# Attention output projection: three high/low products in place of one plain float32 product

## The chip, the cores and the metric

The kernel runs on one core of one Trainium2 chip. The metric is the device time of one execution in microseconds. The profiled execution is one execution of the same program, recorded by the hardware profiler; PE is TensorE, PEld its weight loads, DVE VectorE, ACT ScalarE, POOL GpSimd and SP the engine that issues most DMAs.

## The reference

One transformer block on 4096 tokens (16 batches of 256) of width 256: cross-attention with 16 heads over 77 context rows for each batch, then a mixture of 8 experts with the best 2 for each token.

```
q = (x @ Wq + bq).reshape(bs, n_ctx, HEADS, d)
kv = (data @ Wkv + bkv).reshape(bs, n_data, HEADS, 2 * d)
attn = jax.nn.softmax(scores, axis=-1)
out = jnp.einsum('bhqk,bkhd->bqhd', attn, v).reshape(bs, n_ctx, WIDTH)
return out @ Wp + bp                      # the step that is changed
x = x + xattn(_layernorm(x), ctx, ...)
x = x + ffn(_layernorm(x), ...)           # top 2 of 8 experts, hidden 1024, silu gate, clips
```

All of it is float32. `out @ Wp` is a product of 4096x256 by 256x256.

## The kernel before

The attention part (the first 320 us or so) goes over 32 tiles of 128 tokens, two tiles to a batch. It is written as rounds: in round i every engine does, in a fixed order written out by hand, its share of several tiles at different stages. PE, in round i, does the scores of tile i in two halves, the transposes of the exponentials of tile i-1, the transpose of the attention result of tile i-2 (`transpose_attn`, L1777), in an even round the keys and values of the next batch (`keys_values`, L1844 the keys, L1849 the values product "v"), in an odd round the queries (L1788), the router product (L1833), the projection of tile i-2 (`project`, L1798), and the product of probabilities and values of tile i-1 (L1821). DVE does the two halves of the softmax input (`softmax_input`: L1245 the maxima, L1251 the subtractions) of tile i, then sums for the layer norms (L1266, L1290, L1300), the addition of the projection to x (`make_x1`, L1280), and the division of the attention result (L1311, L1316). ACT evicts the transposes (`attn_t_copy`, L963, for the attention result). Engines wait for each other through semaphores only, so the order in each engine's program and the waits set everything.

The small products that go through PSUM once in a round share two banks, `misc_bank`. `misc_turns()` deals them out in turn: attn, k, v, ... in an even round; attn, q, logits, ... in an odd one. `claim(name, i)` on PE makes a product wait until the one before it in the same bank has been read, and `misc_read` says by which semaphore that is known. Because the banks alternate, the v product of an even round always comes into the bank that held the transposed attention result, and the logits product of an odd round likewise:

```
misc_read = {"ctx": lambda b: (ctx_t_out, b + 1), "attn": lambda i: (attn_t_out, i + 1),
def claim(name, i):
    bank, before = misc[name, i]
    if before:
        e.wait_ge(*misc_read[before[0]](before[1]))
```

In the last rounds (28 to 31) DVE and ACT also split the first expert's weights into a high and a low part (`high_weights`, L1031, on ACT; `low_weights`, L1592, on DVE), and the expert part begins on PE while rounds 32 to 36 drain. The expert part (L1981, L2025) works throughout with such pairs: a number is written as its float32r rounding (high) plus the rest (low), and one product is made of three: high by high, high by low, low by high. The scores (L1743) do so too. The projection doesn't: attn_t and wp are plain float32.

Of the kernel before, what the change touches and what calls it, by code (L numbers as in the profile page):

```python
# [8 lines left out]
F32 = mybir.dt.float32  # L9
# [7 lines left out]
P = 128  # L17
# [237 lines left out]
def build(nc, a, out):  # L255
    with ExitStack() as ctx:
# [8 lines left out]
        def sems(name, n):  # L265
# [44 lines left out]
         gate_out, gate_clipped, silu_made, hid_made, hid_clipped, hid_high, hid_low, y_added,  # L310
         y_clipped, y_scaled, last_mm, last_added, last_clipped, first_found, part_gates, gate_known, token_kept) = (
            sem(n) for n in ("w_high", "w_low", "rows_t_mm", "rows_scaled", "rows_high",
# [3 lines left out]
                             "first_found",  # L316
                             "part_gates", "gate_known", "token_kept"))

# [22 lines left out]
        for name, n in (("early", N_EARLY), ("full", N_LATE), ("half", MAX_HALF),  # L341
# [22 lines left out]
        scope.append(ExitStack())  # L364
        cs = [sb(f"cs{i}", [CTX, D]) for i in range(2)]
        c_t = sb("c_t", [P, DC, CTX])
        k_t = sb("k_t", [P, DC, CTX])
        k_parts = sb("k_parts", [P, 2, DC, CTX], F32R)
# [10 lines left out]
        probs_t = [sb(f"probs_t{i}", [P, KB, P]) for i in range(2)]  # L379
        zeros = sb("zeros", [P, D])  # L380
        qk_bias = sb("qk_bias", [P, 2 * DC])
        bq_scaled = sb("bq_scaled", [P, DC])
        maxes = [sb(f"maxes{i}", [P, HEADS]) for i in range(2)]
        wp = sb("wp", [P, DC, D])
        rows = sb("rows", [P, 4, D])
        bv_row, bp_row, g_row, b_row = (rows[:, i, :] for i in range(4))
        xs = [sb(f"xs{i}", [P, D]) for i in range(XR)]
        attn = [sb(f"attn{i}", [P, D]) for i in range(2)]
        attn_t = [sb(f"attn_t{i}", [P, DC, P]) for i in range(2)]
        recip = [sb(f"recip{i}", [P, HEADS]) for i in range(2)]  # L390
# [44 lines left out]
        misc, (last_on_bank6, last_on_bank7) = misc_turns()  # L435
        misc_read = {"ctx": lambda b: (ctx_t_out, b + 1), "attn": lambda i: (attn_t_out, i + 1),
                     "q": lambda b: (q_out, 2 * b + 2), "proj": lambda i: (x1_made, i + 1),
# [4 lines left out]
        def misc_of(name, i):  # L442
            return misc_bank[misc[name, i][0]]
# [49 lines left out]
        def sync_program(e):  # L493
# [144 lines left out]
            for i in range(FIRST_ROUND, OVERLAP + 2):  # L638
                nb = i // 2 + 1
                batch = 0 <= nb < BATCH  # L640
                if i == EARLY_TILES + 8:
                    e.wait_ge(early_known, 1)
                    load_expert(0)
                    load_matrix(0, 1)
                if 8 <= i + 7 < NT:
                    load_x(i + 7)
                load_rest(i)
                if batch and i % 2:
                    load_values(nb)
                    if nb + 2 < BATCH:  # L650
                        load_ctx(nb + 2)
                if i == EARLY_TILES + 9:
                    load_matrix(0, 0)
                    wait_puts(EARLY_TILES // 2)
                    load_rows(0)
                if i == EARLY_TILES + 10:
                    load_matrix(0, 2)
                    e.wait_ge(q_mm, BATCH)
                    e.wait_ge(v_mm, BATCH)
                    load_expert(1)  # L660
                    load_rows(1)
                if 0 <= i - 2 < NT:
                    store_x1(i - 2)
                if batch and i % 2 == 0:
                    if nb == 0:
                        spread_keys(nb)
                    store_values(nb)
                    if nb:
                        spread_keys(nb)
# [222 lines left out]
        def act_program(e):  # L892
# [66 lines left out]
            def attn_t_copy(i):  # L959
                e.wait_ge(attn_t_mm, i + 1)  # L960
                if i >= 2:
                    e.wait_ge(proj_mm, i - 1)
                e.activation(attn_t[i % 2][:, :, :],  # L963
                             misc_of("attn", i)[:, 0:DC * P].rearrange("p (c k) -> p c k", c=DC),
                             ACTF.Copy).then_inc(attn_t_out, 1)

            def xf_t_copy(i):
# [135 lines left out]
            def round_ops(i):  # L1103
# [5 lines left out]
                if 0 <= i - 2 < NT:  # L1109
                    attn_t_copy(i - 2)  # L1110
                if before:
                    probs_t_copy(i - 1, 1)
# [114 lines left out]
        def dve_program(e):  # L1227
# [80 lines left out]
            def normalized(i):  # L1308
# [5 lines left out]
                if i >= 2:  # L1314
# [3 lines left out]
                                recip[i % 2][:, :].unsqueeze(2).broadcast_to([P, HEADS, HD]),  # L1318
                                ALU.mult).then_inc(attn_made, 1)

            def best_experts(i):
# [210 lines left out]
            def round_ops(i):  # L1532
                even, nb = i % 2 == 0, i // 2 + 1
                batch = 0 <= nb < BATCH
                if 0 <= i < NT:
                    softmax_input(i, 0)
                for w, c in FIRST_PIECES.get(i - 1, []):
                    low_weights(0, w, c)
# [185 lines left out]
        def pe_program(e):  # L1724
# [67 lines left out]
            def project(i):  # L1792
                ps = claim("proj", i)
                e.wait_ge(attn_t_out, i + 1)
                if i == 0:
                    e.wait_ge(f_wp, 32)
                for c in range(DC):
                    mm = e.matmul(ps[:, 0:D], attn_t[i % 2][:, c, :], wp[:, c, :], start=(c == 0),  # L1798
                                  stop=(c == DC - 1))
                mm.then_inc(proj_mm, 1)  # L1800
# [361 lines left out]
```

## Time and profile before

| | |
|---|---|
| measured times | 937.89, 940.01, 942.44 us (median 940.01) |
| profiled execution, span | 941.1 us, 19403 instructions |
| PE busy | 899.3 us, 96% of the span |
| DVE busy | 745.2 us, 79% |
| ACT busy | 652.6 us, 69% |
| POOL busy | 411.4 us, 44% |

The span of the profiled execution is the time to which terms are added here; it lies 1.1 us over the median of the three runs. A busy share is an average over the attention part and the expert part. The end that a matmul record shows is modelled, so how long a group of products holds PE is read from the start of one group to the start of the next.

### The profile page before, as it was taken

Reading aid. Unit: us, or ns where it says so; the run is one execution under the profiler, and the core shown is the slowest. Engines: PE = TensorE matmul, PEld = TensorE weight load, DVE = VectorE, ACT = ScalarE, POOL = GpSimd, SP = SyncE. Lnnn points to the kernel's source line nnn. Section 1 sums busy time; section 2 is a strip of 40 time slices with the busy share of each in tenths; the row PEclk is TensorE's granted clock in tenths of the full one; section 3 lists DMA queues with packets and bytes.
Section 4 is the critical chain, followed back from the end, with each engine's and each line's share of the span. In section 5 each row is a group of like instructions: output and inputs, shape, how many; then the busy total and the mean of one; then the engine's idle time right before and its main releaser. Section 6 shows DMA issues by size and latency. Waiting matters only on the chain.

```text
span 941.1 us, 19403 instructions
## 1 busy us (share of the span) xinstructions
PE 899.3 (96%) x6270; PEld 806.3 (86%) x6270; DVE 745.2 (79%) x1765; ACT 652.6 (69%) x1337; POOL 411.4 (44%) x649
## 2 busy tenths in 40 slices
PE   5999999999999998999999999999999999999994
PEld 4787888888888877888999989899898998998994
DVE  2677878888888888887979888887877877878883
ACT  3566677677767774675877777866776777677773
POOL 3445577677777567330432240505214234052042
PEclk9999999999999999999999999999999999999998
DMA  6232233334246327743756454827817738466442
GB/s 144 56 63 47 52 87 92 72 83 98 58 113 200 113 75 287 203 109 122 216 123 181 134 159 163 240 91 186 298 27 219 273 74 263 164 181 182 136 79 26
DMA packets 132626, 129.19 MB, mean 137 GB/s; under 512 B 59984, under 2 KB 117408, under 8 KB 132384
## 3 DMA queue, kind: packets, MB, share of 16 engines
q1 hardware_dynamic: 119648, 110.36, 38.7%
q0 software_dynamic: 12864, 17.44, 10.1%
q8 instruction: 56, 0.92, 0.4%
q14 instruction: 58, 0.48, 0.2%
HBM read 102.01 MB, written 25.36 MB: 135 GB/s over the span
## 4 chain that ended last, share of the span: by engine, by line
PE 81%; DVE 5%; issue 5%; ACT 3%; POOL 3%; DMA 1%; SPq 0%; another core or an unknown queue 0%; POOLq 0%; DVEq 0%; ACTq 0%
PE bank L1981 36%; PE bank L2025 18%; PE bank L1821 5%; PE bank L1973 3%; PE bank L1743 3%; PE bank L1798 3%; PE bank L1761 3%; PE bank L1788 2%; PE bank L1950 2%; PE bank L2013 2%; PE bank L1844 1%; PE bank L1849 1%; PE bank L1806 1%; DVE maxes L1245 1%; PE bank L1833 1%
## 5 line engine op out<-in xcount | busy, mean ns | idle before, releaser
L851 POOL DMA_INDIRECT out_rows<-yo,token x68 | 114.3, 1680 | 383.0 <-ACT yo L1100 317.5
L1981 PE MATMUL bank<-xh,wh 128*128 128x512 f32 (+1 forms) x672 | 234.5, 349 | 3.3 <-DVE gate_in L1616 2.8
L1981 PE MATMUL bank<-xl,wh 128*128 128x512 f32 (+1 forms) x672 | 228.9, 341 | 0.0
L1981 PE MATMUL bank<-xh,wl 128*128 128x512 f32 (+1 forms) x672 | 228.4, 340 | 0.0
L1592 DVE TENSOR_TENSOR wl<-raw,wh 128x1024 fp32r<-128x1024 f32 x126 | 152.4, 1220 | 13.2 <-ACT wh L1031 11.7
L2025 PE MATMUL bank<-wh,hh 128*128 128x256 f32 x496 | 141.8, 286 | 1.6 <-issue 1.4
L1981 PEld LDWEIGHTS bank<-xh,wh 128*128 128x128 f32 x672 | 128.2, 191 | 17.3 <-DVE gate_in L1616 4.7
L2025 PE MATMUL bank<-wh,hl 128*128 128x256 f32 x496 | 140.5, 283 | 0.4 <-issue 0.4
L2025 PE MATMUL bank<-wl,hh 128*128 128x256 f32 x496 | 140.2, 283 | 0.3 <-issue 0.3
L1981 PEld LDWEIGHTS bank<-xh,wl 128*128 128x128 f32 x672 | 127.8, 190 | 14.9
L1981 PEld LDWEIGHTS bank<-xl,wh 128*128 128x128 f32 x672 | 128.2, 191 | 10.9
L1031 ACT ACTIVATE wh<-raw 128x1024 fp32r<-128x1024 f32 x126 | 131.1, 1054 | 0.2 <-DMA raw<-in_W 0.2
L1636 DVE TENSOR_TENSOR hl<-gate_in,hh 128x512 fp32r<-128x512 f32 x128 | 87.9, 687 | 43.1 <-ACT hh L1094 32.6
L1069 ACT ACTIVATE gate_in<-bank,par 128x512 f32<-128x512 f32 x88 | 60.2, 684 | 61.8 <-PE bank L1981 56.6
L1094 ACT ACTIVATE hh<-gate_in 128x512 fp32r<-128x512 f32 x128 | 80.2, 626 | 28.5 <-DVE gate_in L1629 26.0
L2025 PEld LDWEIGHTS bank<-wh,hh 128*128 128x128 f32 x496 | 94.8, 191 | 5.0 <-issue 2.3
L2025 PEld LDWEIGHTS bank<-wl,hh 128*128 128x128 f32 x496 | 94.8, 191 | 2.5
L2025 PEld LDWEIGHTS bank<-wh,hl 128*128 128x128 f32 x496 | 94.7, 191 | 1.1 <-issue 1.1
L1081 ACT ACTIVATE gate_in<-gate_in 128x512 f32<-128x512 f32 (+1 forms) x144 | 86.1, 598 | 0.0
L798 POOL DMA_INDIRECT z_rows<-z,slot x64 | 68.0, 1063 | 22.2 <-issue 17.7
L1821 PEld LDWEIGHTS bank<-v_blocks,probs_t 128*128 128x128 f32 (+1 forms) x640 | 75.3, 192 | 0.9
L1821 PE MATMUL bank<-v_blocks,probs_t 128*128 128x51 f32 (+2 forms) x640 | 75.2, 274 | 0.0
(198 smaller groups left out, 1887.6 us busy)
## 6 DMA issues: line engine op xcount, KB each, us to landing
raw<-in_W SPq DMA_DIRECT2D x42, 1024.0 KB
raw<-in_Wo SPq DMA_DIRECT2D x25, 1024.0 KB
whole<-in_W SPq DMA_DIRECT2D x8, 1024.0 KB, 8.4
xs<-in_x SPq DMA_DIRECT2D x32, 128.0 KB, 2.6
out_rows<-x SPq DMA_DIRECT2D x32, 128.0 KB, 2.2
shared<-z_rows SPq DMA_DIRECT2D x7, 520.0 KB
bo_row<-in_bo SPq DMA_DIRECT2D x25, 128.0 KB
k_blocks<-k_parts SPq DMA_DIRECT2D x128, 19.2 KB
```

Of the source, the lines that this page charges most:

```text
L798: e.indirect_dma_start(out=z_rows, out_offset=bass.IndirectOffsetOnAxis(ap=slot[:, 2 * p + t, k:k + 1], axis=0), in_=z[p % ZR][:, t, :], i ...
L851: e.indirect_dma_start(out=out, out_offset=bass.IndirectOffsetOnAxis(ap=token[j % 4][:, s:s + 1], axis=0), in_=yo[j % 2][:, s, :], in_offs ...
L1031: e.activation(wh[split_before(j) % 2][:, w, c, :], raw[w][:, c, :], ACTF.Copy).then_inc(w_high, 1)
L1069: e.activation(dst[:, :], ps[:, 0:WIDTH], ACTF.Identity, bias=par[j % PR][:, X_B2 + u:X_B2 + u + 1]).then_inc(gate_out, 1)
L1081: e.activation(gate_in[n % 3][:, 0:w], gate_in[n % 3][:, 0:w], ACTF.Silu).then_inc(silu_made, 1)
L1094: e.activation(dst, hid[n % 3][:, 0:w], ACTF.Copy).then_inc(hid_high, 1)
L1592: e.tensor_tensor(wl[q][:, w, c, :], raw[w][:, c, :], wh[q][:, w, c, :].bitcast(F32), ALU.subtract).then_inc(w_low, 1)
L1636: e.tensor_tensor(hl[n % (HR - 1)][:, :], hid[n % 3][:, :], hh[n % HR][:, :].bitcast(F32), ALU.subtract).then_inc(hid_low, 1)
L1743: mm = e.matmul(score_bank[(u0 + g) % 3][:, 0:HPB * CTX], qs[b % 2][g * HALF:(g + 1) * HALF, m, s * P:(s + 1) * P], k_blocks[b % 2][g * HA ...
L1821: mm = e.matmul(value_bank[:, first * VW:(first + nh) * VW], probs_t[i % 2][0:size, k, :], v_blocks[b % 2][0:size, k, 0:nh, :].rearrange(" ...
L1981: mm = e.matmul(ps[:, h * cols:(h + 1) * cols], ws[split_before(j) % 2][:, w, c, m * P:(m + 1) * P], xx[j % 2][:, c, 0:cols], start=(h == ...
L2025: mm = e.matmul(down_bank[s // 2][:, (s % 2) * D:(s % 2 + 1) * D], hs[:, at:at + P], ws[q][:, 2, m // 4, (m % 4) * D:(m % 4 + 1) * D], sta ...
```

## The change

The projection is made of three float32r products. ACT's copy of the transposed attention result now writes its float32r rounding (`attn_h`); DVE subtracts that from the same PSUM bank (`low_attn`, new, writes `attn_l` and the semaphore `attn_low`). `wp` is split once into `wp_parts` (`high_wp` on ACT in round 0, `low_wp` on DVE in round 1). PE's `project` waits for `attn_low` and issues, for each half of the contraction, high by high, high by low and low by high. The bank that held the transposed attention result counts as read when DVE, not ACT, has read it. To find room, cs, c_t, k_t, wp and zeros are laid into the weight buffers `raw`, which are empty in this part; SP's first loads of expert weights get waits for that.

```diff
-        cs = [sb(f"cs{i}", [CTX, D]) for i in range(2)]
+        cs = [raw[2][0:CTX, 1, i * D:(i + 1) * D] for i in range(2)]
...
+        wp = raw[0][:, 0, 0:DC * D].rearrange("p (c n) -> p c n", c=DC)
...
-        wp = sb("wp", [P, DC, D])
+        wp_parts = sb("wp_parts", [P, 2, DC, D], F32R)
-        attn_t = [sb(f"attn_t{i}", [P, DC, P]) for i in range(2)]
+        attn_h = [sb(f"attn_h{i}", [P, DC, P], F32R) for i in range(2)]
+        attn_l = [sb(f"attn_l{i}", [P, DC, P], F32R) for i in range(2)]
...
-        misc_read = {... "attn": lambda i: (attn_t_out, i + 1),
+        misc_read = {... "attn": lambda i: (attn_low, i + 1),
...
                 if i == EARLY_TILES + 8:
                     e.wait_ge(early_known, 1)
                     load_expert(0)
+                    e.wait_ge(f_dump, 16 * (ROW_HALF // P))
                     load_matrix(0, 1)
                 if i == EARLY_TILES + 9:
+                    e.wait_ge(wp_low, 1)
                     load_matrix(0, 0)
                 if i == EARLY_TILES + 10:
+                    e.wait_ge(v_mm, BATCH)
                     load_matrix(0, 2)
                     e.wait_ge(q_mm, BATCH)
-                    e.wait_ge(v_mm, BATCH)
...
-                e.activation(attn_t[i % 2][:, :, :],
+                e.activation(attn_h[i % 2][:, :, :],
...
+            def high_wp():
+                e.wait_ge(f_wp, 32)
+                e.activation(wp_parts[:, 0, :, :], wp, ACTF.Copy).then_inc(wp_high, 1)
...
+            def low_attn(i):
+                e.wait_ge(attn_t_out, i + 1)
+                if i >= 2:
+                    e.wait_ge(proj_mm, i - 1)
+                e.tensor_tensor(
+                    attn_l[i % 2][:, :, :],
+                    misc_of("attn", i)[:, 0:DC * P].rearrange("p (c k) -> p c k", c=DC),
+                    attn_h[i % 2][:, :, :].bitcast(F32), ALU.subtract).then_inc(attn_low, 1)
...
                 if 0 <= i < NT:
                     softmax_input(i, 0)
+                if i == 1:
+                    low_wp()
+                if 0 <= i - 2 < NT:
+                    low_attn(i - 2)
                 for w, c in FIRST_PIECES.get(i - 1, []):
                     low_weights(0, w, c)
...
             def project(i):
                 ps = claim("proj", i)
-                e.wait_ge(attn_t_out, i + 1)
+                e.wait_ge(attn_low, i + 1)
                 if i == 0:
-                    e.wait_ge(f_wp, 32)
+                    e.wait_ge(wp_low, 1)
                 for c in range(DC):
-                    mm = e.matmul(ps[:, 0:D], attn_t[i % 2][:, c, :], wp[:, c, :], start=(c == 0),
-                                  stop=(c == DC - 1))
+                    for k, (at, w) in enumerate(((attn_h, 0), (attn_h, 1), (attn_l, 0))):
+                        mm = e.matmul(ps[:, 0:D], at[i % 2][:, c, :], wp_parts[:, w, c, :],
+                                      start=(c == 0 and k == 0), stop=(c == DC - 1 and k == 2))
```

On PE, in an even round of the program before (round 2: the last transposes of probabilities, the keys, the v product, the second half of the scores, the projection), with the semaphores that each instruction waits for:

```order
L1761 MATMUL bank<-const,probs 128x128 x3
L1844 MATMUL bank<-c_t,shared 128x77 [waits ctx_t_out,xn_t_out]
L1844 MATMUL bank<-c_t,shared 128x77 x3
L1849 MATMUL bank<-shared,c_t 77x256 [waits attn_t_out]
L1849 MATMUL bank<-shared,c_t 77x256
L1743 MATMUL bank<-k_blocks,q_h 128x308 [waits less_max]
...
L1798 MATMUL bank<-wp,attn_t 128x256 [waits f_wp,attn_t_out,k_out]
L1798 MATMUL bank<-wp,attn_t 128x256
L1821 MATMUL bank<-v_blocks,probs_t 128x34 [waits probs_t_out,attn_made]
```

The same place in the changed program (L1880 is the v product, L1829 the projection):

```order
L1791 MATMUL bank<-const,probs 128x128 x3
L1875 MATMUL bank<-raw,shared 128x77 [waits ctx_t_out,xn_t_out]
L1875 MATMUL bank<-raw,shared 128x77 x3
L1880 MATMUL bank<-shared,raw 77x256 [waits attn_low]
L1880 MATMUL bank<-shared,raw 77x256
L1773 MATMUL bank<-k_blocks,q_h 128x308 [waits less_max]
...
L1829 MATMUL bank<-wp_parts,attn_h 128x256 [waits wp_low,attn_low,k_out]
L1829 MATMUL bank<-wp_parts,attn_h 128x256
L1829 MATMUL bank<-wp_parts,attn_l 128x256
L1829 MATMUL bank<-wp_parts,attn_h 128x256 x2
L1829 MATMUL bank<-wp_parts,attn_l 128x256
L1852 MATMUL bank<-v_blocks,probs_t 128x34 [waits probs_t_out,attn_made]
```

The instructions stand where they stood; the projection is six instead of two, and the v product waits for DVE's new subtraction where it waited for ACT's copy.

On DVE, the same round before (maxima and subtractions of the first half, the sums of xf, the addition that reads v, the second half):

```order
L1245 TENSOR_REDUCE maxes<-bank 128x4 [waits scores_mm]
L1251 TENSOR_TENSOR probs<-bank,maxes 128x308 [waits max_found] x2
L1266 BN_STATS stats<-xf 128x6 [waits xf_made]
L1338 TENSOR_TENSOR v_sb<-bank,rows 77x16x16 [waits f_vstore1,v_mm]
L1245 TENSOR_REDUCE maxes<-bank 128x4 [waits scores_mm] x2
```

And in the changed program:

```order
L1257 TENSOR_REDUCE maxes<-bank 128x4 [waits scores_mm]
L1263 TENSOR_TENSOR probs<-bank,maxes 128x308 [waits max_found] x2
L1342 TENSOR_TENSOR attn_l<-bank,attn_h 128x256 [waits proj_mm,attn_t_out]
L1278 BN_STATS stats<-xf 128x6 [waits xf_made]
L1364 TENSOR_TENSOR v_sb<-bank,rows 77x16x16 [waits f_vstore1,v_mm]
L1257 TENSOR_REDUCE maxes<-bank 128x4 [waits scores_mm] x2
```

The new subtraction stands behind the first half of the softmax input of the same round, so it can't run before those four operations are done.

## Rows read from the trace of the kernel before

**Rows 1.** The attention part as one stretch: length, busy us (count) of each engine, PE clock, DMA share, GB/s.
```profile
40.00:320.00 280.00, 271.83 (x2133) 234.87 (x2133) 228.59 (x792) 197.65 (x531) 185.23 (x345) 1.00 0.36 83
```

**Rows 2.** Timeline of PE, even round: start us, us, engine, line, operation.
```profile
161.20 0.42 PE L1743 MATMUL bank<-k_blocks,q_h 64*128 64x308 f32 x2
161.45 0.31 PE L1743 MATMUL bank<-k_blocks,q_l 64*128 64x308 f32 x2
161.59 0.30 PE L1743 MATMUL bank<-k_blocks,q_h 64*128 64x308 f32 x2
161.83 0.44 PE L1806 MATMUL bank<-const,xn 128*128 128x128 f32 x2
...
164.30 1.04 PE L1849 MATMUL bank<-shared,c_t 128*77 128x256 f32 x4
165.28 0.41 PE L1743 MATMUL bank<-k_blocks,q_h 64*128 64x308 f32 x2
...
166.54 1.11 PE L1798 MATMUL bank<-wp,attn_t 128*128 128x256 f32 x4
167.49 0.17 PE L1867 MATMUL bank<-both,tri 128*128 128x16 bf16 x1
```

**Rows 3.** Timeline of DVE, around the same even round.
```profile
160.23 0.42 DVE L1280 TENSOR_TENSOR x<-bank,xs 128x256 f32<-128x256 f32 x1 [0.19 <-PE bank L1798]
...
164.65 0.85 DVE L1251 TENSOR_TENSOR probs<-bank,maxes 128x308 f32<-128x308 f32 x2
165.43 0.41 DVE L1266 BATCH_NORM_STATS2 stats<-xf 128x6 f32<-128x256 f32 x1
```

**Rows 4.** Timeline of ACT, the eviction of the transposed attention result, same round.
```profile
163.81 0.39 ACT L963 ACTIVATE attn_t<-bank 128x256 f32<-128x256 f32 x1
```

**Rows 5.** Timelines of PE and DVE, first and last of eleven such rounds.
```profile
91.37 1.04 PE L1849 MATMUL bank<-shared,c_t 128*77 128x256 f32 x4
92.75 0.41 PE L1743 MATMUL bank<-k_blocks,q_h 64*128 64x308 f32 x2 [0.33 <-DVE probs L1251]
92.22 0.85 DVE L1251 TENSOR_TENSOR probs<-bank,maxes 128x308 f32<-128x308 f32 x2
272.00 1.03 PE L1849 MATMUL bank<-shared,c_t 128*77 128x256 f32 x4
272.58 0.85 DVE L1251 TENSOR_TENSOR probs<-bank,maxes 128x308 f32<-128x308 f32 x2
```

**Rows 6.** Groups by line (count, busy us, mean ns, idle before).
```profile
L1280 DVE TENSOR_TENSOR x<-bank,xs 128x256 f32<-128x256 f32 x32 | 13.2, 413 | 8.8 <-PE bank L1798 7.2 <-remote 1.6
```

**Rows 7.** Waits from 40 to 320 us: who for whom, us in total, times, longest.
```profile
PE bank L1743 <- DVE probs L1251: 2.1, 5, 0.5
```

**Rows 8.** Timeline of PE, expert part: float32r products of 256 columns in a row.
```profile
402.08 0.28 PE L2025 MATMUL bank<-wl,hh 128*128 128x256 f32 x1
402.20 0.28 PE L2025 MATMUL bank<-wh,hl 128*128 128x256 f32 x1
```

**Rows 9.** Timelines of ACT and DVE, round 31.
```profile
301.74 0.38 ACT L963 ACTIVATE attn_t<-bank 128x256 f32<-128x256 f32 x1
300.45 2.36 DVE L1592 TENSOR_TENSOR wl<-raw,wh 128x1024 fp32r<-128x1024 f32 x2 [0.61 <-issue]
307.27 0.50 PE L1981 MATMUL bank<-xh,wh 128*128 128x512 f32 x1 [0.44 <-DVE probs L1251]
```

**Rows 10.** PE after a long gap; then stretches: length, PE busy (count), clock.
```profile
334.06 0.18 PE L1867 MATMUL bank<-both,tri 128*128 128x16 bf16 x1 [1.95 <-ACT logits L979]
334.00:336.00 2.00, 1.94 (x16) 0.93 0.13 46
336.00:338.00 2.00, 2.00 (x9) 0.50 0.25 87
338.00:340.00 2.00, 2.00 (x8) 0.71 0.23 75
```

**Rows 11.** Timeline of PE: a gap in the attention part after which the clock stayed.
```profile
26.72 0.41 PE L1743 MATMUL bank<-k_blocks,q_h 64*128 64x308 f32 x2 [1.34 <-DVE probs L1251]
```

More of the change, by code:

```diff
@@ L310, in build @@
          gate_out, gate_clipped, silu_made, hid_made, hid_clipped, hid_high, hid_low, y_added,
-         y_clipped, y_scaled, last_mm, last_added, last_clipped, first_found, part_gates, gate_known, token_kept) = (
+         y_clipped, y_scaled, last_mm, last_added, last_clipped, first_found, part_gates, gate_known, token_kept,
+         wp_high, wp_low, attn_low) = (
             sem(n) for n in ("w_high", "w_low", "rows_t_mm", "rows_scaled", "rows_high",
@@ L316, in build @@
                              "first_found",
-                             "part_gates", "gate_known", "token_kept"))
+                             "part_gates", "gate_known", "token_kept", "wp_high", "wp_low",
+                             "attn_low"))
         banks = [ctx.enter_context(nc.psum_tensor(f"bank{i}", [P, 512], F32)) for i in range(8)]
@@ L364, in build @@
         scope.append(ExitStack())
-        cs = [sb(f"cs{i}", [CTX, D]) for i in range(2)]
-        c_t = sb("c_t", [P, DC, CTX])
-        k_t = sb("k_t", [P, DC, CTX])
+        cs = [raw[2][0:CTX, 1, i * D:(i + 1) * D] for i in range(2)]
+        c_t, k_t = (raw[2][:, 0, i * DC * CTX:(i + 1) * DC * CTX].rearrange(
+            "p (c k) -> p c k", c=DC) for i in range(2))
+        wp = raw[0][:, 0, 0:DC * D].rearrange("p (c n) -> p c n", c=DC)
         k_parts = sb("k_parts", [P, 2, DC, CTX], F32R)
@@ L379, in build @@
         probs_t = [sb(f"probs_t{i}", [P, KB, P]) for i in range(2)]
-        zeros = sb("zeros", [P, D])
+        zeros = raw[1][:, 0, 0:D]
         qk_bias = sb("qk_bias", [P, 2 * DC])
@@ L435, in build @@
         misc, (last_on_bank6, last_on_bank7) = misc_turns()
-        misc_read = {"ctx": lambda b: (ctx_t_out, b + 1), "attn": lambda i: (attn_t_out, i + 1),
+        misc_read = {"ctx": lambda b: (ctx_t_out, b + 1), "attn": lambda i: (attn_low, i + 1),
                      "q": lambda b: (q_out, 2 * b + 2), "proj": lambda i: (x1_made, i + 1),
@@ L1110, in round_ops @@
                     attn_t_copy(i - 2)
+                if i == 0:
+                    high_wp()
                 if before:
@@ L1319, in normalized, with low_wp @@
                                 ALU.mult).then_inc(attn_made, 1)
+            def low_wp():
+                e.wait_ge(wp_high, 1)
+                e.tensor_tensor(wp_parts[:, 1, :, :], wp, wp_parts[:, 0, :, :].bitcast(F32),
+                                ALU.subtract).then_inc(wp_low, 1)
+            def low_attn(i):
[6 more added lines that the diff above has]
+                    attn_h[i % 2][:, :, :].bitcast(F32), ALU.subtract).then_inc(attn_low, 1)
             def best_experts(i):
```

## The prediction

> **What bounds the kernel now.** I read the busy shares first, then the attention part as one stretch, then the timelines of PE, DVE and ACT side by side in one even round. In the attention part PE is busy 271.83 of 280 us at full clock, DVE 228.59, ACT 197.65 [rows 1]. So PE sets the time there, and DVE has a fifth left. A share doesn't say where that fifth lies, and in the even rounds it doesn't lie where the new operation goes. In the round that begins at 161.20, PE starts the v product at 164.30 and goes straight on to the second half of the scores at 165.28 [rows 2]. ACT had evicted the transposed attention result by 163.81 + 0.39 = 164.20 [rows 4]. That eviction is all that v waits for today. DVE is behind: it added the last projection to x at 160.23, worked without a gap, did the two subtractions of the first softmax half from 164.65 on, and got to its next operation (L1266) at 165.43 [rows 3], 1.13 us after v had started. Nobody waits for that now. The addition at 160.23 itself had waited on PE (the bracket in its row), so DVE's position is tied to PE's projection of the odd round: if PE is held, DVE is held too and doesn't catch up. That matters for the sum.
>
> **The change, part by part.** The diff reads as an edit of the projection. What the order of instructions shows is more: the v product of each even round now waits for DVE's subtraction, because both share a bank, and that subtraction stands behind the first softmax half on DVE.
>
> *The new wait.* The subtraction (128x256, one operand in PSUM, one in SBUF) has no row of its own; the nearest is the addition of the projection to x, same size, same sources, 413 ns [rows 6]. Its slot is where L1266 starts now, 165.43. It ends at 165.84. From the end of a DVE operation to the product that it releases I take 0.06 us: the first of two subtractions started at 92.22 and takes about half of the pair's 0.85 with overlap, some 0.46, and the scores started at 92.75 [rows 5]. So v starts at 165.90 instead of 164.30, 1.60 later. Put generally: the wait is (end of the subtraction pair minus start of v) + 0.40; here 165.50 - 164.30 + 0.40. I read this difference in all fourteen even rounds that have both products. In eleven (batches 5 to 15) DVE ends later than v starts: 1.70, 0.74, 1.86, 1.76, 1.20, 1.16, 1.27, 1.33, 1.89, 1.34, 1.43 us, the first and the last being 93.07 - 91.37 and 273.43 - 272.00 [rows 5]. Sum 15.7, plus 11 x 0.40 = 4.4: 20.1 us. Of this PE already loses a part just behind v, where the scores wait for the subtractions: in the attention part 2.1 us over 5 places [rows 7], of which I take 1.8 as lying in these rounds (0.33 of it at 92.75 [rows 5]). A later v swallows it: 20.1 - 1.8 = **18.3 us**. In two of the three earlier rounds DVE is on time but ACT's eviction ends only 0.1 us ahead of v, and the chain eviction, 0.06, 0.41, 0.06 puts v back by 0.4 each: **0.8 us**. The third has room.
>
> Do the delays add up over the rounds, or does DVE catch up while PE waits? Behind v, DVE's next work waits for PE (the addition to v, the second softmax half, the addition to x). From the addition to x (160.23) to the slot (165.43) are 5.2 us of DVE work without idle time [rows 3], and that addition waits for PE's projection. So each round's delay is passed on whole. What could shorten it is the time from the projection to that addition, in which I see DVE idle in many odd rounds; if that lag weren't carried along, the reciprocal (which waits for the values product of PE) would lead, and about 0.4 us would be saved in nine rounds, 3.8 us. I keep that for the range.
>
> *The projection on PE.* Four float32 records hold PE from 166.54 to 167.49, 0.95 us [rows 2]. A float32r product of 256 columns holds it 0.12 us (402.08 to 402.20) [rows 8]; six are 0.72. But the neighbours (router and values product) are plain float32, and crossing costs: in the scores, two groups inside a run of float32r are 0.14 apart (161.45 to 161.59), the last one is 0.24 from the float32 transpose behind it, and the first 0.25 from the second [rows 2]. That is 0.11 going in and 0.10 coming out: 0.72 + 0.21 = 0.93, a gain of 0.02, **about 0** over 32. Ends: with no crossing cost 32 x 0.23 = 7.4 us gained; with 0.95 + 0.05 for waiting on the low part, 1.6 lost. The Trainium skill, "TensorE: Matmul & The Clock Gate", section "Back-to-back issue gap", gives 262 cycles for 256 columns at full clock, an estimate of 0.109 us each; by it the six would take 0.66, and the sum would be 2 us lower. The row with weight loads beside it says 0.12, and I go by the row.
>
> *Round 31.* Here ACT evicts the attention result late, at 301.74 + 0.38 = 302.12, behind the weight splits. DVE meets the new subtraction before its two weight splits, which now start at 300.45 [rows 9]. It must wait: 302.12 + 0.06 + 0.41 = 302.6, and the splits start 2.1 us later. Behind them come the second softmax half and then PE's first expert product, which at 307.27 already waited 0.44 for DVE [rows 9]. **2.1 us**, whole. In rounds 29, 30, 32 and 33 DVE has about 1 us of idle time behind the new operation: nothing, and up to 0.4 each if that cover is gone.
>
> *Odd rounds.* The subtraction there waits for ACT's eviction and then fills DVE's idle time before the second softmax half, about 1 us; the logits product, which shares the bank, comes later. Nothing; if the cover is gone some 0.1 us in each of 16 rounds, 1.6.
>
> *Edits at nothing.* ACT's eviction keeps its shape (0.39 [rows 4]). The two splits of wp (128x512 each) fall in rounds 0 and 1, where DVE and ACT idle between halves of the softmax; without that cover 0.7 us each, once. The waits added to SP's weight loads are for things over long before. The moved buffers are as large as before.
>
> *The clock.* PE at 334.06 had idled 1.95 us, and soon after the granted clock fell to 0.50, 1.2 GHz, while PE was busy throughout: means of 0.93, 0.50 and 0.71 over three stretches of 2 us [rows 10]. What was lost is 2 x (0.07 + 0.50 + 0.29) = 1.7 us. After a gap of 1.34 us (26.72) the clock stayed at 2.4 GHz [rows 11]. My gaps are 1.2 to 2.3 us, between and beyond these rows. I put one fall into the sum, **1.7 us**, and eleven into a rival.
>
> Sum: 18.3 + 0.8 + 0 + 2.1 + 1.7 = 22.9 us on the profiled span of 941.1, 964.0; that span lies 1.1 over the median of the runs, so **963 us**, 2.4% slower.
>
> **The rivals.** *The clock falls in most of the new gaps.* Each costs PE 1.7 us in a stretch where PE leads again: ten falls more than in the sum, 963 + 17 = 980 us. For it: the 1.95 us row. Against it: the 1.34 us row, and that PE is dense around my gaps. Chance 0.15.
>
> *A smaller stall.* The waits are there, but the lag behind the odd projection isn't passed on (3.8 less) and crossing is cheaper (up to 7.4 less): 952 to 956. Chance 0.06.
>
> *No stall, faster.* One mechanism: DVE reaches the new subtraction early enough that v doesn't wait. Then only the projection counts: 32 x 0.23 = 7.4 off, 932.6 us. It decides at DVE being about 1.6 us earlier in eleven rounds. For it: the three early rounds, where DVE isn't late. Against it: eleven of fourteen rounds, and DVE gets 32 operations more, not fewer. Chance 0.06.
>
> *No change that can be told.* A measurement of this kernel tells 0.5% from nothing, 4.7 us. It would need the waits to be real but halved, and the projection to give back 7 us. Chance 0.05.
>
> **How the numbers follow.** The full stall with few falls of the clock has 0.68, and by its bounds (3.8 down, 7.4 down at most together with it in part, 3 up for lost cover and one or two more falls) lies in 955 to 970. The range takes in the smaller stall and the clock rival: 950 to 982. Slower by over 0.5%: 0.68 + 0.15 + 0.06 = 0.89; faster 0.06; same 0.05.
>
> **What would show it.** In the profile after: the v product with idle time before it, released by DVE's new subtraction, 1.2 to 2.3 us in each even round of batches 5 to 15, and from one such round to the next some 1.6 us more than before; PE busy well under its 97% in the attention part; the projection's six products in 0.9 us; the first expert product some 20 us later; the expert part behind it as long as before. The prediction is wrong if DVE's subtraction ends before v is due, if the additions to x move forward relative to PE while PE waits, if the six products take near 0.7 us with no crossing cost, or if the clock row shows 0.5 through the attention part.

## The result, and the profile after

The changed kernel takes 968.81 us (median of four runs: 957.91, 965.60, 972.02 and 972.82), the kernel before 941.23 in the same session: slower by 27.6 us; the forecast was 963. The fourth run lies over 1.5% above the fastest and is left out of the comparison: by the other three, median 965.60, the loss is 24.4 us, ratio 1.026, 95% interval 1.022 to 1.031.

The profile is of the run of 972.02 us, the longest of those three. Its page (span 970.2), against a granted clock row of nearly all nines before:

```profile
span 970.2 us, 19594 instructions
PE 913.4 (94%) x6334; PEld 822.5 (85%) x6334; DVE 761.5 (78%) x1798; ACT 655.1 (68%) x1338; POOL 410.4 (42%) x649
PEclk9999979797999999999999999999999999999998
```

The same stretch as in [rows 1], and then the stretches from the first expert product to the end, of this kernel (columns: length, busy us and count of PE, PEld, DVE, ACT, POOL, PE clock, DMA share, GB/s):

```profile
40.00:320.00 280.00, 259.85 (x1952) 228.28 (x1951) 218.58 (x747) 177.73 (x480) 165.45 (x318) 0.92 0.31 71
...
338.22:970.20 631.98, 612.06 (x4086) 560.47 (x4086) 510.18 (x964) 447.20 (x790) 215.26 (x265) 0.99 0.54 161
```

and of the kernel before:

```profile
307.27:941.10 633.83, 612.59 (x4082) 561.00 (x4082) 509.78 (x962) 447.39 (x790) 214.72 (x265) 0.99 0.55 161
```

From the first expert product on nothing grew (631.98 against 633.83), so all of the loss lies ahead of it, in the attention part: PE is busy 259.85 instead of 271.83 of 280 us, and its clock there is 0.92 instead of 1.00. Two things, then: idle time and clock.

A "gap" is idle time of PE ahead of one product; a "fall" is a stretch in which the granted clock is 0.50.

**The idle time.** Whom PE waits for from 40 to 345 us (us in total, times, longest), against [rows 7]:

```profile
PE bank L1880 <- DVE attn_l L1342: 16.0, 13, 2.0
PE bank L2012 <- DVE probs L1263: 2.3, 1, 2.3
PE bank L1829 <- ACT q_t L938: 1.8, 8, 0.6
```

L1880 is the v product, which had no wait before; with 0.24 us ahead of the third v product, at 37.88 us, the sum is 16.3. Timelines of PE and DVE in one such round, the answer to [rows 2, 3]:

```profile
125.69 1.01 PE L1875 MATMUL bank<-raw,shared 128*128 128x77 f32 x8
128.53 1.09 PE L1880 MATMUL bank<-shared,raw 128*77 128x256 f32 x4 [1.83 <-DVE attn_l L1342]
126.51 0.86 DVE L1257 TENSOR_REDUCE maxes<-bank 128x4 f32<-128x308 f32 x2
127.29 0.86 DVE L1263 TENSOR_TENSOR probs<-bank,maxes 128x308 f32<-128x308 f32 x2
128.06 0.41 DVE L1342 TENSOR_TENSOR attn_l<-bank,attn_h 128x256 fp32r<-128x256 f32 x1
```

The subtraction ends at 128.47, v starts at 128.53: the 0.06 us and the 0.41 us of the forecast. The next rows are the projection at full clock, and the first expert product:

```profile
145.65 0.48 PE L1829 MATMUL bank<-wp_parts,attn_h 128*128 128x256 f32 x2
145.97 0.28 PE L1829 MATMUL bank<-wp_parts,attn_l 128*128 128x256 f32 x1
146.09 0.40 PE L1829 MATMUL bank<-wp_parts,attn_h 128*128 128x256 f32 x2
146.33 0.28 PE L1829 MATMUL bank<-wp_parts,attn_l 128*128 128x256 f32 x1
146.45 0.75 PE L1852 MATMUL bank<-v_blocks,probs_t 128*128 128x34 f32 x6
338.22 0.80 PE L2012 MATMUL bank<-xh,wh 128*128 128x512 f32 x1 [2.26 <-DVE probs L1263]
```

Six products hold PE from 145.65 to 146.45, 0.80 us, where the two of before held it 0.95 [rows 2]. The last of them starts at 146.33 and the plain float32 values product 0.12 later: going out of float32r into that product costs nothing. The 0.80 is met within 0.02 in all 29 projections at full clock.

**The clock.** Stretches of PE around two of the fourteen v products, both released after a long gap:

```profile
128.00:130.00 2.00, 1.47 (x8) 0.96 (x10) 1.15 (x4) 1.49 (x5) 1.66 (x3) 0.93 0.00 0
130.00:142.00 12.00, 12.00 (x62) 11.20 (x59) 6.41 (x24) 3.99 (x13) 5.38 (x9) 0.50 0.30 65
142.00:146.00 4.00, 4.00 (x23) 3.14 (x23) 1.99 (x8) 3.16 (x7) 3.50 (x8) 0.83 0.46 107
173.00:175.00 2.00, 1.88 (x10) 1.27 (x10) 0.82 (x3) 1.47 (x5) 1.63 (x3) 0.77 0.00 0
175.00:186.00 11.00, 11.00 (x57) 10.30 (x54) 6.16 (x22) 3.50 (x12) 4.99 (x8) 0.50 0.28 60
```

After the gap of 1.83 us at 128.53 PE works without a pause for 12 us at 0.50, 1.2 GHz, and then comes back. (1 - clock), summed over windows of 1 us, gives 6.8 us lost in this one fall, and the same for those that follow the gaps of 2.00 at 173.12 and at 217.67 us. Shorter falls lose 1.7 each, like the one in [rows 10]. Ahead of its first expert product the kernel before lost 1.7 us in this way, the changed one 25.8. The short falls have no rule that these traces show. In the changed kernel one begins at 27.3 us and one at 297.0, behind these two gaps:

```profile
25.76 0.41 PE L1773 MATMUL bank<-k_blocks,q_h 64*128 64x308 f32 x2 [1.33 <-DVE probs L1263]
296.30 0.41 PE L1773 MATMUL bank<-k_blocks,q_h 64*128 64x308 f32 x2 [1.55 <-DVE q_l L1297]
```

The first is the gap of [rows 11], behind which the kernel before had kept its clock; and the one short fall in the attention part of the kernel before, at 35.4 us, has no gap over 1 us in the 8 us ahead of it. Behind the other gaps at v, up to 1.55 us, nothing fell.

**The account.** "Net" is a stretch without what its clock lost. The v product of a batch is the mark; the third is at 39.12 us before and 37.88 after, the sixteenth at 272.00 [rows 5] and 301.85.

| us, after minus before | time | clock | net |
|---|---|---|---|
| start to third v | -1.2 | +1.7 | -2.9 |
| third to sixteenth v: 232.9, then 264.0 | +31.1 | +22.2 | +8.9 |
| sixteenth v to first expert product: 35.3, then 36.4 | +1.1 | +0.2 | +0.9 |
| expert part: 633.8, then 632.0 | -1.9 | -0.4 | -1.5 |
| span | +29.1 | +23.7 | +5.4 |

So four fifths of what was lost in this execution is clock, and one fifth is what is left of the waits after what the projection gives back. It is the share of this execution: the run of 957.91 us had a mean granted clock of 0.983 where this one had 0.968, an estimate of 16 us lost (0.017 of 956) instead of 31. Nor can "net" be read to the microsecond. Up to the third v the time doesn't follow the clock at all: this and the ten other changed executions that lost 3.4 us or more there took 37.0 to 39.4 us, the kernel before, e4 and e6, which lost 1.7, took 38.9 to 40.8. The experiments take the loss apart.

### The profile page after: what moved, and what is told of

It is laid out like the page before. It is cut to its first block, busy times and chain, and to the rows that moved or that the text cites. A ratio compares the mean times of both kernels' runs of the same rounds, so it can differ in the third digit from the quotient of the medians.

```text
span 970.2 us, 19594 instructions
## 1 busy us (share of the span) xinstructions
PE 913.4 (94%) x6334; PEld 822.5 (85%) x6334; DVE 761.5 (78%) x1798; ACT 655.1 (68%) x1338; POOL 410.4 (42%) x649
## 4 chain that ended last, share of the span: by engine, by line
PE 76%; DVE 10%; issue 5%; ACT 5%; POOL 2%; SPq 1%; DMA 1%; DVEq 0%; ACTq 0%; POOLq 0%
PE bank L2012 34%; PE bank L2056 17%; PE bank L1852 7%; PE bank L2004 3%; PE bank L1773 3%; PE bank L1829 3%; PE bank L1791 2%; PE bank L1880 2%; PE bank L2044 1%; DVE maxes L1257 1%; PE bank L1818 1%; PE bank L1981 1%; DVE probs L1263 1%; PE bank L1864 1%; PE bank L1837 1%
## 5 line engine op out<-in xcount | busy, mean ns | idle before, releaser
L1852 PE MATMUL bank<-v_blocks,probs_t 128*128 128x51 f32 (+2 forms) x640 | 81.4, 287 | 0.0
L1852 PEld LDWEIGHTS bank<-v_blocks,probs_t 128*128 128x128 f32 (+1 forms) x640 | 80.2, 205 | 0.0
L804 POOL DMA_INDIRECT z_rows<-z,slot x64 | 69.4, 1084 | 21.3 <-issue 17.7
```

The costliest lines, as they stand in the source:

```text
L804: e.indirect_dma_start(out=z_rows, out_offset=bass.IndirectOffsetOnAxis(ap=slot[:, 2 * p + t, k:k + 1], axis=0), in_=z[p % ZR][:, t, :], i ...
L1852: mm = e.matmul(value_bank[:, first * VW:(first + nh) * VW], probs_t[i % 2][0:size, k, :], v_blocks[b % 2][0:size, k, 0:nh, :].rearrange(" ...
```

## Experiments

The measure beside the ratio is, from each profile, the stretch from the third to the sixteenth v: time, clock lost, net. Before: 232.9, 0.0, 232.9. Changed: 264.0, 22.2, 241.8. Theory: the wait of v costs its 16 us and brings the falls. Rivals: the products; DVE's added operations as such; a clock that falls without the gaps. e1 to e4, e5 to e8 and e9 to e12 ran together, each four on another chip and beside the kernel before (943.85, 946.55 and 944.06 us); its own stretch was profiled once, in the first session. So the ratios against the kernel before, and comparisons within one group of four, are the safe ones. The ratio is worked out from the runs beside each other and isn't that of the two medians. The profiles of e2, e3, e8 and e11 are of the fastest run, 3 to 7 us under the median, and most of the other runs have a lower granted clock.

**e1_products_only.** The bank is free with ACT's eviction, and there is no subtraction.

```diff
-        "attn": lambda i: (attn_low, i + 1)
+        "attn": lambda i: (attn_t_out, i + 1)
-    low_attn(i - 2)
-    e.wait_ge(attn_low, i + 1)
+    e.wait_ge(attn_t_out, i + 1)
-    ((attn_h, 0), (attn_h, 1), (attn_l, 0))
+    ((attn_h, 0), (attn_h, 1), (attn_h, 0))
```

> The changed kernel without DVE's low part: the projection still makes six float32r products, but the third of each three reads the high part again, the bank counts as read when ACT has evicted it, and DVE does no subtraction. (The low part of the attention result is left out of the sum.) Theory A, the loss is the wait of the v product for DVE: the wait is gone, the six products hold PE 0.80 us where the four float32 records held it 0.95, so 32 x 0.15 = 4.8 us under the kernel before: 936 us (933 to 940). Theory B, the six products themselves cost (crossing between float32 and float32r): 941 to 950. PE clock in the attention part 1.0 by A.

965.46 us, ratio 1.025 (1.021 to 1.030). The time can't be used: the third product was high by high once more, so the projection was counted twice, the routing changed, and the expert part took 653.2 us. The attention part can: no wait at v, stretch 234.9, clock 6.6, net 228.4.

**e5_products_only_again.** As e1 with `(attn_h, 1)` as the third; what is left out is the attention result's low part.

> As the first products-only kernel, but the third product of each three is high by low once more instead of high by high, so that the projection stays of its true size and the tokens go to the same experts. (The low part of the attention result is left out of the sum.) The wait theory: no wait before v, v to v 17.4 us in the steady part instead of 17.7, projection 0.80 us: 936 us (932 to 940), or up to 943 if the clock falls two or three times more than before. The theory that the products cost: 945 and more.

944.61 us, ratio 0.9996 (0.996 to 1.004): no change, where I had expected 936, or 943 at most. Stretch 237.3, clock 5.5, net 231.8, which is 1.1 under before; e1's is 4.5 under. The attention parts of e1 and e5 are the same work, so these 3.4 us are what net can differ by between two executions. Twenty-six projections at 0.15 us would give 3.9. So the products cost nothing that shows and give back 1 to 4.5 us net, and in the whole time that was eaten: this profile lost 10.2 us to the clock before the first expert product, in falls of 1.7 and 3.4 us.

**e2_wait_only.** The other half: plain float32 projection, subtraction and wait kept.

```diff
-    for k, (at, w) in enumerate(((attn_h, 0), (attn_h, 1), (attn_l, 0))):
-        mm = e.matmul(ps[:, 0:D], at[i % 2][:, c, :], wp_parts[:, w, c, :], ...
+    mm = e.matmul(ps[:, 0:D], attn_h[i % 2][:, c, :], wp_parts[:, 0, c, :], ...
```

> The changed kernel with the plain float32 projection of before (2 products of a float32 copy of the transposed result and a float32 copy of wp), but with DVE's subtraction and the v product waiting for it, as in the changed kernel. Theory A: the whole loss is there, waits before v of some 16 us, 2 us in round 31, and falls of the clock on top: 960 to 978 us. Theory B, the products are the loss: under 950 us.

964.44 us, ratio 1.024 (1.019 to 1.030). Who waits for whom on PE:

```profile
PE bank L1879 <- DVE attn_l L1342: 14.1, 13, 2.0
PE bank L2011 <- DVE probs L1263: 2.1, 1, 2.1
```

Stretch 249.7, clock 3.4, net 246.2: 13.3 over before with 14.1 us of waits, less 1.8 that were lost at the scores before. The wait is passed on whole, and 1.0 more. The changed kernel has this and the cheaper projection, 246.2 - 3.9 = 242.3, and its own net is 241.8. What e2 doesn't have are the long falls, though three of its gaps are 1.89, 1.79 and 1.98 us long: behind the first two the clock stays at 1.00, behind the third is a short fall. Its runs' granted clocks are 0.979 to 0.986.

**e6_low_twice.** The suspected cost doubled: DVE does the subtraction twice, and the bank waits for the second.

> The changed kernel with DVE's subtraction done twice over (the second after the first), so that the bank is released some 0.35 to 0.45 us later in every round. If each delay is passed on whole: the waits before v add up to some 21 to 22 us instead of 16.3, v to v about 0.4 us longer than 18.9, and with the same falls of the clock 974 us (968 to 980). If DVE catches up while PE waits: waits of 17 us or less, time as of the changed kernel.

990.9 us, ratio 1.042 (1.033 to 1.050).

```profile
PE bank L1885 <- DVE attn_l L1346: 21.3, 11, 2.6
```

The waits are as expected, 21.3 us. Net 248.8, 7.0 over the changed kernel for a second subtraction of 0.41 us in each of the fourteen batches of the stretch (5.7). The time is above the expected one, 968 to 980, by the clock: 36.5 us lost before the first expert product, 27 of it in four falls of 5 to 8.5 us. Yet behind two of its gaps, 2.51 and 2.17 us (186.74 and 206.64), the clock stayed at 1.00.

**e4_filled_gap.** The wait kept, and the gap filled with products that nothing reads.

```diff
+FILL = 24
...
+    if b >= 4:
+        e.wait_ge(probs_t_out, 6 * b - 8)
+        stay_busy(FILL, trans_bank[(6 * b - 7) % 2])
     ps = claim("v", b)
```

> The changed kernel with 24 dummy bf16 products of 128 columns (some 1.6 us of PE) ahead of the v product from batch 4 on, so that PE is busy where it would wait. Theory D, the gaps before v are what lets the clock fall: clock 1.0 in the attention part and only the waits are left, 941 + 16 + 2 - 5 = 954 to 959 us, with little spread between runs. Rival: the falls come from something else; clock 0.92 there and 965 to 973 us.

958.25 us, ratio 1.014 (1.008 to 1.020); granted clocks 0.987 to 0.993. The clock row of its page, and the same place as above in the timeline of PE:

```profile
PEclk9999999999999899999999999999999999999998
...
129.65 1.50 PE L1914 MATMUL bank<-ones 128*128 128x128 bf16 x24
131.64 1.09 PE L1884 MATMUL bank<-shared,raw 128*77 128x256 f32 x4 [0.49 <-DVE attn_l L1343]
```

The v product is as late as before (19.39 us behind the v product of the batch before, 19.45 in the changed kernel), net is even 3.6 us worse (245.4), but the clock loses 1.7 us in the stretch instead of 22.2. PE gained no useful work, and against the kernel before the loss is 1.4% instead of 2.6% (4.2% in e12). That speaks for the gaps as what lets the clock fall. But the changed kernel wasn't run on this chip, and e2, beside it, with its gaps open, lost only 3.4 us in the stretch. What the runs beside each other on this chip show is smaller: granted clocks of 0.984 to 0.992 for the kernel before, as high with the gaps filled, 0.979 to 0.986 in e2 with them open.

**e12_changed_again.** The changed kernel itself, in the session of e9 to e11.

> The changed kernel once more, to see how its falls of the clock vary. Gaps at v of 14 to 17 us in sum as in its first profile, since they come from the order of work; the time lost to the clock in the first 360 us is what may differ, between 10 and 30 us; whole time 955 to 973 us.

984.12 us (982.27 to 986.45), ratio 1.042 (1.038 to 1.047), 15 us over its first median and over the 955 to 973 expected. Stretch 272.3, clock 30.5, net 241.8: the net is the same to a tenth, closer than two executions can be counted on to agree, and all of the difference is clock. Its waits at v sum to less (11.8 us against 16.3), since at 1.2 GHz PE comes later to v, and DVE is ready; twice PE waits for ACT ahead of the projection instead, 1.66 and 1.63 us. Behind a gap of 2.18 us at 174.49 the clock stayed; a fall at a gap of 2.24 us:

```profile
194.49 1.14 PE L1880 MATMUL bank<-shared,raw 128*77 128x256 f32 x2 [2.24 <-DVE attn_l L1342]
194.00:196.00 2.00, 1.51 (x4) 0.84 (x4) 0.78 (x3) 1.63 (x5) 1.77 (x3) 0.56 0.00 0
196.00:206.00 10.00, 10.00 (x51) 8.78 (x50) 5.07 (x20) 1.71 (x5) 3.23 (x6) 0.50 0.19 31
```

**e3_bank_by_act.** The wait taken away and all the arithmetic kept: ACT copies the bank to a buffer in SBUF, and makes the high part from it; DVE subtracts in SBUF; the bank is free with ACT's copy.

```diff
-    e.activation(attn_h[i % 2][:, :, :], misc_of("attn", i)[:, 0:DC * P]...
+    e.activation(attn_t, misc_of("attn", i)[:, 0:DC * P]...).then_inc(attn_t_out, 1)
+def high_attn(i):
...
+    e.activation(attn_h[i % 2][:, :, :], attn_t, ACTF.Copy).then_inc(attn_high, 1)
...
-    misc_of("attn", i)[:, 0:DC * P]..., attn_h[i % 2][:, :, :].bitcast(F32)
+    attn_t, attn_h[i % 2][:, :, :].bitcast(F32)
```

> The changed kernel, complete, but ACT evicts the transposed result once as float32 (this frees the bank) and makes the high part from that copy in SBUF behind the next eviction of probabilities; DVE subtracts in SBUF. DVE and PE do the same work as in the changed kernel, ACT has 32 copies more. Theory A (the wait for the bank): no wait before v, no gaps, clock 1.0; 941 - 4.8 + 2 for the wait in round 31 = 938 us (934 to 945). Theory C (DVE's added work is the loss, wherever it waits): 955 us or more.

954.95 us, ratio 1.014 (1.010 to 1.019). The wait at v is gone as expected, the time isn't back: 938 was expected. Net 233.6 in the stretch, 0.8 over before; clock 6.8; and 38.9 us instead of 35.3 from the sixteenth v to the first expert product. PE's waits are now many small ones:

```profile
PE bank L1842 <- ACT q_t L940: 5.8, 12, 0.9
PE bank L1786 <- DVE probs L1276: 2.9, 6, 0.8
PE bank L2025 <- DVE probs L1276: 2.3, 1, 2.3
```

ACT has 32 copies more here, and PE waits 5.8 us for it ahead of the projection where the changed kernel waits 1.8. So e3 takes away the wait and the long gaps, and puts ACT's work in their place; it doesn't show what DVE's work costs. The granted clocks of its four runs are 0.965 to 0.984, and the profile is of the one with 0.984.

**e11_work_only.** DVE's added work without anyone waiting for it: e5's products, and a subtraction from SBUF that nothing reads.

> The six products, all with the high part of the attention result (the low part of it is left out of the sum, which changes the result slightly), and DVE does one subtraction of the same size per tile at the place of the new one, but from SBUF, and neither the v product nor the projection nor the bank waits for it. Rival theory (DVE's added work costs by itself): 955 us or more. My theory (only the wait costs): as the products alone, within 0.5% of the kernel before, since DVE has a fifth of its time left in this part.

955.65 us, ratio 1.012 (1.009 to 1.015): not the time of the kernel before, which I had expected, but what I had written down for the rival. It is 11.6 us over the kernel before. The profile is of the fastest run, 948.96 us: stretch 239.8, clock 3.4, net 236.4, 4.6 over e5 and 8.0 over e1. Behind the sixteenth v come 1.6 more (36.6 against 35.0 net), since in round 31 DVE still waits for ACT there. The group from 40 to 320 us, and one of the operations:

```profile
L1343 DVE TENSOR_TENSOR attn_l<-attn_h 128x256 fp32r<-128x256 f32 x30 | 15.6, 521 | 12.1 <-ACT attn_h L970 8.5 <-issue 3.6
125.13 0.85 DVE L1343 TENSOR_TENSOR attn_l<-attn_h 128x256 fp32r<-128x256 f32 x1
```

It takes 521 ns in the mean (median 426) and at times 0.85, where the real one from PSUM takes 419. So the rival has a part, and not a small one: 32 operations on DVE cost 1.2% of the whole time (e5 had a ratio of 0.9996) even when nothing waits for them, 5 to 8 us of it net in the attention part. The real operations may cost less, since these are longer; by how much was not tested.

**e8_v_late.** The v product behind the second half of the scores and the last transposes, its addition on DVE behind the second softmax half.

> The changed kernel, complete, with the v product moved on PE behind the second half of the scores and the last transposes of probabilities (and DVE's addition to it behind the second half of the softmax input), from round 2 on. The wait theory: v no longer waits, the scores ahead of it wait 0.5 to 0.9 us for DVE's first subtraction in the same rounds, v to v about 18.0: 944 us (938 to 952). If DVE's added work itself is the limit: 955 or more.

964.86 us, ratio 1.022 (1.014 to 1.030); my expectation, 944, failed. Whom PE waits for, from 40 to 330 us:

```profile
PE bank L1775 <- DVE probs L1263: 8.9, 9, 1.7
PE bank L1831 <- DVE v_sb L1364: 6.1, 10, 0.6
```

The wait went from v to the scores behind it (8.9) and to the projection, whose bank now comes free later (6.1). Net 245.1, worse than the changed kernel.

**e9_between.** In even rounds the subtraction stands between the maxima and the two subtractions of the first softmax half.

```diff
     e.tensor_reduce(maxes[i % 2][:, hs], view, AXX, ALU.max).then_inc(max_found, 1)
+if m == 0 and i % 2 == 0 and i >= 2:
+    low_attn(i - 2)
 for g in range(2):
...
-if 0 <= i - 2 < NT:
+if 0 <= i - 2 < NT and (i % 2 or i >= NT):
     low_attn(i - 2)
```

> The changed kernel, complete, but in even rounds DVE makes the low part between the two maxima and the two subtractions of the first softmax half, instead of behind them. The v product is then released some 0.85 us earlier (two subtractions), the second half of the scores is no later than v makes it. My theory (the wait of v is the loss, and the clock falls behind its gaps): gaps at v of 0.3 to 1.1 us in eleven rounds, sum 7 to 9 us instead of 16.3, v-to-v near 18.3, few long falls of the clock, whole time 945 to 957 us. Rival (32 additional operations on DVE cost the time, wherever they stand): as the changed kernel, 964 to 970 us.

956.56 us, ratio 1.014 (1.010 to 1.019), against 1.042 for e12 in the same session. DVE in one round, and the sum of PE's waits:

```profile
126.83 0.86 DVE L1257 TENSOR_REDUCE maxes<-bank 128x4 f32<-128x308 f32 x2
127.61 0.42 DVE L1344 TENSOR_TENSOR attn_l<-bank,attn_h 128x256 fp32r<-128x256 f32 x1
127.94 0.86 DVE L1265 TENSOR_TENSOR probs<-bank,maxes 128x308 f32<-128x308 f32 x2
PE bank L1882 <- DVE attn_l L1344: 8.4, 11, 1.4
```

Half of the waits are gone (8.4), no gap at v is over 1.4 us, and of the long falls none is left: clock 6.8 in the stretch where e12, on the same chip, lost 30.5, and granted clocks of 0.975 to 0.982 in its six runs against 0.955 to 0.965. This pair is the best evidence that the long gaps bring the long falls. Net 239.1: 2.7 better than e12, not 8. That the subtraction now makes the softmax later would explain it; no run shows that by itself.

**e7_weights_first** and **e10_between_weights_first.** The subtraction behind the weight splits instead of ahead of them: in e7 wherever there are splits, in e10 in round 31 and on top of e9.

> The changed kernel with DVE's new subtraction behind the splits of the first expert's weights in rounds 29 to 31 instead of ahead of them. By my term for round 31 the wait of 2.3 us before the first expert product goes back to about 0.4 to 0.7, and the time drops by 1.5 to 2; if the wait has another cause it stays 2.3.

> As e9, and in round 31 alone the low part is made behind the two weight splits instead of ahead of them. The wait of the first expert product (2.3 us) goes, against a small wait of the projection of that round (0.6 us where this was tried with all rounds): 1.5 to 2.3 us less than e9, 943 to 955 us. If the round-31 term is covered by something else, the same time as e9.

e7 has one run, 989.5 us, with 38.4 us lost to the clock; its time says nothing, but the wait of the first expert product is gone. Its first long fall, of 13.7 us, begins 1.3 us behind a gap of 1.57 us (91.31). e10: 955.64 us, ratio 1.012 (1.007 to 1.018), the same as e9 within the intervals; the wait is gone (2.27 in e9), the projection of that round waits 0.6, and from the sixteenth v to the first expert product net falls from 36.5 to 34.6, 1.9 us where 1.5 to 2.3 were expected. The whole time doesn't show it (0.9 us).

No version beats the kernel before.

## Why the prediction was right, and which of its steps were not

The sign and the place were right, and of the cause the wait at v; 963 lies 6 us under the median of all four runs and 2.6 under that of the three compared, inside the range. But that the sum came so near is luck: its errors cancelled. The waits and the projection came out about 11 us cheaper than forecast, the clock in the profiled execution 22 us dearer.

- **The wait of v** (forecast 18.3 + 0.8 net of the 1.8). The mechanism and the price of one are as said: 0.41 + 0.06, in batches 5 to 15. The eleven sum to 15.6 where 20.1 were forecast (0.67 to 2.00 us each, where 1.2 to 2.3 were), three earlier ones to 0.7. e2 shows 13.3 net. The step that was off is "each round's delay is passed on whole": what PE waits is passed on, e2 shows that, but DVE's lateness itself is some 0.4 a round smaller than before. In e2, whose clock hardly fell, the reciprocal on DVE waits 12.0 us for PE's values product where it waited 9.7 (both from 40 to 320 us): it leads in more rounds, as in the 3.8 us that I kept for the range alone. That this is all of the difference is argued, not shown.
- **The projection** (forecast 0). It gives back 0.15 us each, 4.8 over 32. The crossing cost of 0.10 coming out was taken from a transpose behind the scores; the values product doesn't pay it. The end that I named (7.4) was too far, the value that I took too near.
- **Round 31** (forecast 2.1). 2.26 - 0.44 = 1.8, and e10 gets it back.
- **The clock** (forecast 1.7). This is the term that was mis-sized: 24 us in the first profile, 36 in e12's (37.6 against 1.7 before the first expert product). The rival gave it 0.15 and 17 us, as ten short falls. What came is another form: behind each of the three gaps of 1.83 to 2.00 us the clock is at 1.2 GHz for 13.7 us, 6.8 us lost each. "After a gap of 1.34 us the clock stayed", which the step leaned on, isn't a bound either: behind the same gap, 1.33 us in the changed kernel, it fell.
- **DVE's work at no cost** (in odd rounds, and as such). e11 puts it at 1.2% of the time, with a longer operation. In the changed kernel it can't be told from the wait, so part of what is called the wait's here may be DVE's work.

Shown: that the wait of v holds PE back (e2, e6), that the products don't (e5), and that the changed kernel's two profiles differ by clock alone (e12, same net). Well supported, by e9 against e12 on one chip, is that the long falls come with the long gaps at v. Not shown: that a long gap is enough. e2, e6 and e12 have gaps of 1.79 to 2.51 us without a fall, and e7 has a long fall behind one of 1.57. Open: what decides it, whether the chip or the float32r products have a part (the four executions with long falls, of the changed kernel twice, e6 and e7, have both the wait and the float32r products, and e6, e7 and e12 ran on other chips than e2 and e4), how the loss divides between the wait and DVE's work, and why the start up to the third v was 2.9 us shorter net than before, in all the derived kernels but e4 and e6 too.

## What to carry to other kernels

Look at which semaphore frees a shared bank before costing an edit by its arithmetic: here six cheap products replaced two dear ones, and the loss came from one more reader of the bank, standing behind a softmax on another engine. When a change opens gaps of 1.5 to 2 us in a dense TensorE stream, don't price them at their length alone: compare kernels by time less what the clock lost, and take several runs, since the same program with the same net varied by 15 us between two sessions. An engine that is 82% busy, as DVE here, need not have a free slot for 32 operations: a share doesn't say who waits for what stands behind them.

## What the runs showed of the hardware that was not expected

- TensorE at 1.2 GHz for 12 us on end while PE is 100% busy (130 to 142 us), after gaps of 1.83 and 2.00 us in a dense stream; 6.8 us lost each time. The Trainium skill, "TensorE: Matmul & The Clock Gate", section "A second HAM failure mode: psum-queue depth-cycling", tells of a clock that goes to and fro where PE idles briefly and often between groups of products. By that rule, too, the changed kernel would lose more than its gaps, and the traces here agree in part: 22.2 us with the gaps, 1.7 with them filled (e4), but 3.4 with gaps of up to 1.98 us in e2.
- A float32r product directly ahead of a plain float32 one with a 34-column result costs no crossing time (146.33 to 146.45), where 0.10 us was read ahead of a float32 transpose.
- The DVE subtraction took 404 to 426 ns each time with one operand in PSUM (mean 419). With both in SBUF (e11) the median is 426 too, but nine of the 32 took 0.55 to 0.96 us. What holds those up was not looked for.
